# Attention scores computed in four 32-column tiles of TensorE, values product in halves, one output bank for two head groups

## The reference

```python
x = L0_attn_x                                   # 8 x 512 x 128 floats
# attention: 16 heads of dimension 8
h = layernorm(x)
q, k, v = h@Wq.T+bq, h@Wk.T+bk, h@Wv.T+bv       # each 8, 512, 16 heads, 8
a = softmax(einsum('bqhd,bkhd->bhqk', q, k) / sqrt(8))
a = a * head_mask[None, :, None, None]
x = x + einsum('bhqk,bkhd->bqhd', a, v).reshape(8, 512, 128) @ Wo.T + bo
# feed-forward: one shared expert and 8 routed ones (128 -> 512 -> 128), 2 of 8 per token
y = layernorm(x)
probs = softmax(y @ Wr); topk_p, topk_i = top_k(probs, 2); topk_p /= sum(topk_p)
x = x + gelu(y@Wfc_s+b)@Wproj_s+b + sum over the 2 experts of topk_p * (gelu(y@Wfc[e]+b)@Wproj[e]+b)
```

## Time and profile before

| what | value |
|---|---|
| median of three runs | 700.45 us (699.07 to 701.12) |
| profiled execution, its own time | 700.0 us |
| its span, first to last instruction | 698.2 us |
| one batch of attention, in the steady state | 50.3 us |
| attention, first exponential of batch 0 to the end of batch 7 | 76.7 to 472.6 us of the span |
| PE, DVE, ACT, POOL busy over the span | 634, 540, 438, 257 us |

### The profile page before, as it was taken

How to read it: one execution, slowest core, us unless ns; L and a number is a source line. 1 busy time by engine, 2 the same in 40 slices (tenths; PEclk the granted TensorE clock), 3 DMA queues, 4 the chain that set the end, 5 groups by cost and what they waited for, 6 DMA issues and landing times.

```text
span 698.2 us, 13370 instructions
## 1 busy us (share of the span) xinstructions
PE 633.9 (91%) x3934; PEld 324.6 (46%) x3976; DVE 540.3 (77%) x1180; ACT 437.9 (63%) x953; POOL 256.6 (37%) x386
## 2 busy tenths in 40 slices
PE   1766799999999999999999999997979999999996
PEld 1441222323323323323332332323779999998965
DVE  6998778888998998988989989822656666666558
ACT  0881467777687787787787787793425555555541
POOL 6766200020430420421521512506464555454541
PEclk9996799999999999999999999999999999999998
DMA  5399594411311212212221121000112222212174
GB/s 151 93 335 349 126 237 107 115 46 36 92 44 43 83 43 68 69 45 63 63 64 48 58 69 48 21 1 31 47 50 66 66 65 63 68 59 62 47 246 127
DMA packets 67611, 61.28 MB, mean 88 GB/s; under 512 B 16250, under 2 KB 58106, under 8 KB 67562
## 3 DMA queue, kind: packets, MB, share of 16 engines
q1 hardware_dynamic: 63242, 51.79, 26.7%
q0 software_dynamic: 4320, 8.89, 3.8%
HBM read 35.76 MB, written 24.62 MB: 86 GB/s over the span
## 4 chain that ended last, share of the span: by engine, by line
PE 63%; DVE 14%; issue 7%; SPq 5%; POOL 4%; ACT 4%; DMA 3%; DVEq 0%; ACTq 0%; POOLq 0%; another core or an unknown queue 0%
PE ps L1183 13%; PE ps L1172 13%; PE ps L1154 12%; PE ps L1357 10%; PE ps L1369 8%; DVE mx L827 6%; POOL slots L514 2%; DVE x_sb L1097 2%; SPq L295 2%; DMA q_op<-mxT 2%; PE ps L1309 1%; DVE o_t L835 1%; PE ps L1209 1%; PE ps L1317 1%; SPq L305 1%
## 5 line engine op out<-in xcount | busy, mean ns | idle before, releaser
L676 ACT ACTIVATE probs<-ps 128x512 f32<-128x512 f32 x512 | 278.8, 595 | 102.5 <-PE ps L1172 87.8
L827 DVE TENSOR_REDUCE mx<-ps 128x2 f32<-128x1024 f32 x256 | 304.0, 1212 | 42.8 <-PE ps L1154 37.5
L1154 PE MATMUL ps<-k_op,q_op 96*128 96x512 bf16 x512 | 181.5, 394 | 19.2 <-DVE mx L827 7.0
L1172 PE MATMUL ps<-q_op,k_op 128*128 128x512 bf16 x470 | 179.0, 387 | 2.2 <-DMA q_op<-mxT 1.5
L1172 PEld LDWEIGHTS ps<-q_op,k_op 128*128 128x128 bf16 x512 | 49.6, 98 | 187.5 <-ACT probs L676 127.7
L1183 PE MATMUL ps<-probs,v_op 128*32 128x512 f32 x1024 | 136.0, 604 | 0.5 <-issue 0.2
L723 ACT ACTIVATE probs<-ps,b_cur 128x128 f32<-128x128 f32 x284 | 81.4, 368 | 75.7 <-PE ps L1357 65.3
L577 POOL DMA_INDIRECT results<-rest,row_id x71 | 73.9, 1041 | 75.1 <-DVE rest L1041 57.1
L514 POOL DMA_INDIRECT slots<-route_sb,slot_u x64 | 67.0, 1046 | 75.1 <-ACT probs L676 50.8
L1357 PE MATMUL ps<-xn,qk 128*128 128x128 f32 x568 | 79.2, 284 | 3.7 <-DVE xn L1034 1.7
L1154 PEld LDWEIGHTS ps<-k_op,q_op 96*128 96x128 bf16 x512 | 49.5, 99 | 61.7 <-DVE mx L827 27.6
(11 more groups left out here) (135 smaller groups left out, 591.8 us busy)
## 6 DMA issues: line engine op xcount, KB each, us to landing
q_op<-q_scr SPq DMA_DIRECT2D x96, 96.0 KB
k_op<-k_scr SPq DMA_DIRECT2D x96, 96.0 KB
w_sb<-in_W SPq DMA_DIRECT2D x18, 256.0 KB, 4.0
probs<-slots SPq DMA_DIRECT2D x71, 64.5 KB, 1.9
k_scr<-probs SPq DMA_DIRECT2D x16, 256.0 KB, 3.7
q_scr<-probs SPq DMA_DIRECT2D x8, 384.0 KB, 3.1
k_scr<-probs SPq DMA_DIRECT2D x8, 384.0 KB, 3.6
k_scr<-probs SPq DMA_DIRECT2D x16, 128.0 KB, 3.1
```

The source lines that it names most:

```text
L676: nc.scalar.activation(probs[:, i, j, :], ps[:, BK_S + j % key_banks(b, hg), :], ACT.Exp, scale=float(D) ** -0.5).then_inc(s_exp, 1)
L827: nc.vector.reduce_max(mx[:, slot % 2, 2 * p:2 * p + 2], ps[:, bank:bank + 2, :], AX.X).then_inc(s_max, 1)
L1154: last = nc.tensor.matmul(ps[:, BK_A + a % 4, :], q_op[hg][0:SH, j, P * i:P * (i + 1)], k_op[hg][0:SH, j, :], start=True, stop=True)
L1172: nc.tensor.matmul(ps[:, BK_S + j % key_banks(b, hg), :], k_op[hg][:, j, P * i:P * (i + 1)], q_op[hg][:, j, :], start=True, stop=True).the ...
```

## The change

- Every bf16 score matmul (`row_scores`, `key_scores`) becomes four, each with 32 stationary columns, that write four blocks of 32 partitions (`QUARTERS`). The moving operand (512 columns) is the same for all four. `project_out` is cut in the same way, and `max_rows` becomes a matmul with 32 stationary columns.
- `pv` is cut in two halves of 256 queries, eight calls per head group at the steps `PV_SLOTS`, so one half in every second step; `ROW_TILES` now gives two row tiles to steps 0 and 2 of each four.
- Two head groups share bank 6: the ones and values of odd groups lie 16 columns further in `v_op`, and DVE empties the bank once for both. The head mask is multiplied into `wo_sb` once, ahead, by POOL.
- DVE gives up `residual` for batches 0 to 6 and the update of the running count: ACT copies the projection from PSUM to `rest` (L684, step 5 of group 1), POOL adds it (L519 of the changed file) and updates the count (L525).
- `Y_STEPS`, `YT_STEP`, the router's step and the place of `ln2_stats` move.

```diff
-        PV_LAG, MX_STEP, YT_STEP = 11, 7, 13
-        Y_STEPS = (-1, 3, 7, 11)
+        MX_STEP, YT_STEP = 7, 14
+        Y_STEPS = (3, 6, 9, 12)
+        AP_STEP = -11
+        ROUTER_STEP, ROUTER_PAIRS = 3, (2, 3, 4, 5)
-        ROW_TILES = ((0,), (1, 2), (3,), ())
+        ROW_TILES = ((0, 1), (), (2, 3), ())
+        PV_SLOTS = ((11, 12, 13, 15, 17, 19, 21, 23), (9, 11, 13, 15, 17, 19, 21, 23))
+        QUARTERS = [slice(32 * c, 32 * c + 32) for c in range(P // 32)]
...
+            def residual(b):
+                if b == 0:
+                    pool.wait_ge(s_xbo, B)
+                pool.wait_ge(s_apc, b + 1)
+                sl = x_sb[:, b * NT:(b + 1) * NT, :]
+                nc.gpsimd.tensor_tensor(sl, sl, projected[:, :].rearrange("p (n c) -> p n c", c=C), ALU.add).then_inc(s_x2, 1)
...
+            def copy_projection(b):
+                act.wait_ge(s_ap, b + 1)
+                wait(act, s_x2, b)
+                nc.scalar.activation(projected[:, :], ps[:, BK_M, :], ACT.Copy).then_inc(s_apc, 1)
...
-                    nc.vector.scalar_tensor_tensor(out=o_all[:, :, hg, :], in0=o_t[:, :, 1:1 + D],
-                                                   scalar=mask_sb[:, hg:hg + 1],
-                                                   in1=o_rec[:, :].unsqueeze(2).to_broadcast([P, S // 32, D]),
-                                                   op0=ALU.mult, op1=ALU.mult).then_inc(s_onrm, 1)
+                    nc.vector.tensor_tensor(o_all[:, :, 2 * pair:2 * pair + 2, :], both[:, :, :, 1:1 + D],
+                                            o_rec[:, :, :].unsqueeze(3).to_broadcast([P, S // 32, 2, D]),
+                                            ALU.mult).then_inc(s_onrm, 1)
...
-                        if 3 <= p < 7 and hg > 0:
-                            out_norm(b, hg - 1, p - 3)
+                        if 3 <= p < 7 and hg == 2:
+                            out_norm(b, 0, p - 3)
...
-                last = nc.tensor.matmul(ps[:, BK_A + a % 4, :], q_op[hg][0:SH, j, P * i:P * (i + 1)], k_op[hg][0:SH, j, :],
-                                        start=True, stop=True)
+                for c in QUARTERS:
+                    last = nc.tensor.matmul(ps[c, BK_A + a % 4, :], q_op[hg][0:SH, j, P * i + c.start:P * i + c.stop],
+                                            k_op[hg][0:SH, j, :], start=True, stop=True)
...
+                cols = slice(S // 2 * half, S // 2 * (half + 1))
...
                 for j in range(J):
-                    last = nc.tensor.matmul(ps[32 * j:32 * j + 32, BK_O, :], v_op[:, hg, i, j, :], probs[:, i, j, :],
-                                            start=(i == 0), stop=(i == NT - 1))
-                last.then_inc(s_pv, 1)
+                    last = nc.tensor.matmul(ps[32 * j:32 * j + 32, BK_O, cols], v_op[:, hg, i, j, :], probs[:, i, j, cols],
+                                            start=(hg % 2 == 0 and i == 0 and half == 0),
+                                            stop=(hg % 2 == 1 and i == NT - 1 and half == 1))
+                if half == 1:
+                    last.then_inc(s_pv, 1)
```

More of the change, by code:

```diff
@@ L1293, in _ @@
             sequences(attend)
[L1294 to L1295 removed]
+            for k in range(2 * NT):
+                if PV_SLOTS[(HG - 1) % 2][k] >= J * NT:
+                    pv(B - 1, HG - 1, k // 2, k % 2)
             for i in range(NT):
```

134 lines of the change are left out of this document (75 added, 59 removed).

## The result

The changed kernel takes 697.18 us (median of 16 runs, 694.69 to 701.20) against 700.15 (16 runs, 699.07 to 701.12): a ratio of 0.9965, 95% interval 0.9952 to 0.9978. So it is faster by 0.35%, where 3.8% was forecast. The profiled execution took 696.87 us with a span of 695.0.

What follows compares the result with a forecast made beforehand. PE was taken as the bound, busy 49.2 of 50.3 us a batch. Batches 1 to 6 gave 21.6 us, batch 0 2.7, batch 7 1.8 and 0.3: 26.4 together, from 700.0 to a 674 us median, range 662 to 703.

Steps and rivals of the forecast that it cites:

- Edit 1: Attention scores in quarters on PE: 0.22 us a set, cycle 2.95 to 2.61 us, 5.4 us less a batch, 0.7 paid back.
- Rival B: PE not fed fast enough for some 830 records a batch, deciding at 61 ns each: slower, 709 or 733 us; chance 0.15.
- C: Rival: sets of quarters at 0.26 us eat all that PE saves, no change at 700 us; chance 0.05.
- D: Rival: quarters do not run side by side, 0.66 us more a set, 1300 us; chance 0.03.
- Edits 2 and 3: Attention: halves and row tiles shrink ACT's waits at no PE cost; DVE falls from 45.1 to 42.0 us a batch.
- The 1.1 us that I charged to group 0 for VectorE: Group 0 of each batch: DVE needs 11.6 us against PE's 10.4 plus 0.1, making a batch 46.7 us.
- Edit 4: Work moved to ACT and POOL is hidden; scales come 3.3 us into group 2, ACT wants them at about 3.2.
- rival A: Gain partly given back: sets cost 0.24 us or scales come 2 us late for ACT; 685 to 688 us; chance 0.16.
- the sum: Whole kernel: six batches at 3.6 us, batch 0 and both halves of batch 7 added, 26.4 us less in all.
- the half batch: First half of batch 7 in attention: 1.8 us less.
- batch 0: First batch of attention: 2.7 us less, between half and all of 3.6, as its first groups may wait for something else.
- the second half of batch 7: End of attention, without row scores and bounded by ACT: 0.3 us less.

Runs made afterwards that it cites:

- e3: Changed kernel with normalising activations at steps 6, 8, 10, 12 instead of 3, 6, 9, 12: 664.41 us, ratio 0.9624, where the kernel before took 689.55.
- e4: Changed kernel with the last batch's output projection as four whole-array matmuls instead of sixteen of 32 columns: 670.94 us, ratio 0.9731, on an early chip.
- e14: Changed kernel with VectorE's statistics one pair of maxima earlier, normalising steps unaltered: 686.30 us, ratio 0.9844, on a late chip.
- a0: Changed kernel unaltered, measured once more on a late chip: 696.41 us, ratio 0.9951 to the kernel before.
- e7: Changed kernel with normalising at steps 6, 8, 10, 12 and the last projection as four whole-array matmuls: 687.72 us, ratio 0.9805, on a late chip.
- a0c: Changed kernel unaltered, measured again on another late chip: 694.36 us, ratio 0.9928 to the kernel before.
- e15: Changed kernel with statistics one pair of maxima earlier and the last projection as four whole-array matmuls: 685.07 us, ratio 0.9793, on a late chip.
- c1: Kernel before with its 64 scatters moved out of attention to behind it (another output): 765.83 us, ratio 1.1106, on an early chip.

## Why the prediction was wrong, step by step

- **Edit 1** held: sets at 0.22 us, a cycle of 2.60 (2.61 said), the passages at 0.09 to 0.14 us. Rival B was wrong: 201 records in 10.7 us are 53 ns each, under the 61 at which it decides. Nor does the supply set even that pace: the 32 records of the projection (e3's L1250) take 1.08 us in all, under 34 ns each. C and D fell with it.
- **Edits 2 and 3** held in sum: with no late signal and no late scales (e3) a batch takes 46.54 us, 46.7 said, and ACT's waits for key scores fall from 10.3 to 4.2 us a batch; VectorE is busy 42.8 us in the four windows (42.0), ACT 40.3 (38.6). The 1.1 us that I charged to group 0 for VectorE did not fall there (10.7 us, 11.6 said); VectorE is idle there for just 0.2 us, and for 1.0 in group 1, so it probably carries the surplus over. The sum came out right partly by luck, because group 2, which I had left to PE, takes 11.93 with PE busy for 11.55.
- **Edit 4**, "hidden by a hair; each us by which it is late costs one in each batch": late by 0.9 us, and it cost 0.9 to 1.1 in each of seven batches, 6.8 us (groups 2 of e4 against e3). The scales came when I said, 3.2 us into group 2 (3.3 said). The term that was mis-sized is when ACT asks for them: its four exponentials follow each other at 0.6 us, so it is ready 2.4 us into the group, not 3.2 (e14's first normalisation starts there, with the scales ready). The mechanism and its price stood in the text; it is part of rival A.
- **The step that failed** is the sum, which multiplied the 3.6 us of one undisturbed batch by six, and the half batch likewise, and took the part behind attention as unchanged, as if a signal always came as fast as in the earlier trace rows. The scatters appear in it only as POOL's busy time, 14.2 us a batch and harmless; what they do to TensorE's signals was put at nothing. On the chips of the first measurement they hold them up, by up to 1.3 us in the short cycle, which costs 2.2 to 2.5 us a batch of the 3.6.

The account against the forecast's 26.4 us (span before and after: 3.1 gained, 23.3 missing), in differences between the traces. Missing: in batches 2 to 6, groups 0 and 1 take 122.7 us where 5 x 22.2 are undisturbed, 11.7; the same in batch 7, 2.3; the part behind the last exponential is 4.3 longer; late scales 6.8; a start 1.2 us later (it varies by 2 us between runs); the rest of the second half of batch 7, 0.7. Against these, batch 0 is better by 1.7 than I took it, and the undisturbed batches by 2.0 in all. Late signals are thus 14.0 us inside attention, and with those behind it some 16 to 18 of the 23 us. The tail's share is the least certain part: POOL begins its scales there 3.6 us later than before, but whole-array matmuls took back only 2.1 us (a0 to e7) and 2.3 (a0c to e15), and on the two other late chips the changed kernel's tail is 228.7 and 228.6 us.

On an early chip the change should take e3's 664.4 + 6.8 = 671 us, near e4's time, or 0.973 of the kernel before: 18 or 19 us of the 26.4. That is an estimate, and the unaltered kernel was not measured there.

Open: what a late chip has that an early one hasn't, and by which way a scatter holds up TensorE's signals (its issue on GpSimd and its transfers were only moved together). The quarters were never tried without the halves, nor VectorE's lighter load alone. On late chips some semaphore records are missing, so the counts of late signals are lower bounds. All executions carried the profiler; whether one without it shows the same wasn't tried.

## What to carry to other kernels

A stage shortened until its engines hand over without slack pays in full for every late signal that slack used to hide; look in the trace for what runs beside it (here GpSimd's scatters) and compare a batch that has it with one that hasn't, before multiplying one cycle's gain by the number of cycles. Keep TensorE in one column-tiled form through a whole stage or not at all: each passage cost 0.09 to 0.14 us here, and every half-converted stream was slower than the kernel before. A hand-over that is computed to be met by a tenth of a us should be moved by one step at once: here that cost nothing and gave back 7 us.

## What the hardware showed that I had not expected

Late chips lose time behind attention as well, in either kernel, and there with whole-array matmuls alone. The 71 scatters of results by line: the kernel before on the late chip of the first measurement, and on an early one (c1, which is the same kernel behind attention but for the scatters moved there); the changed kernel, and e3.

```profile
L577 POOL DMA_INDIRECT results<-rest,row_id x71 | 73.9, 1041 | 75.1 <-DVE rest L1041 57.1
```

```profile
L572 POOL DMA_INDIRECT results<-rest,row_id x71 | 71.7, 1010 | 67.0 <-DVE rest L1035 49.1
```

```profile
L602 POOL DMA_INDIRECT results<-rest,row_id x71 | 73.4, 1033 | 76.3 <-DVE rest L1071 58.4
```

```profile
L602 POOL DMA_INDIRECT results<-rest,row_id x71 | 71.5, 1008 | 67.6 <-DVE rest L1071 49.8
```

The scatters themselves differ by 25 to 31 ns each, but POOL waits 8.1 and 8.7 us more between them. The timelines show by what. The first layer of an expert, whole-array fp32 matmuls with a scatter beside them, and the activation that reads them, in the kernel before on the late chip:

```profile
530.05 0.98 POOL L577 DMA_INDIRECT results<-rest,row_id  x1 [0.31 <-issue]
530.26 1.06 PE L1357 MATMUL ps<-xn,qk 128*128 128x128 f32 x8
...
531.76 1.14 ACT L723 ACTIVATE probs<-ps,b_cur 128x128 f32<-128x128 f32 x4 [1.55 <-PE ps L1357]
```

The same in e3, on an early chip:

```profile
508.91 0.96 POOL L602 DMA_INDIRECT results<-rest,row_id  x1 [0.30 <-issue]
509.40 1.06 PE L1399 MATMUL ps<-xn,qk 128*128 128x128 f32 x8
510.05 1.14 ACT L756 ACTIVATE probs<-ps,b_cur 128x128 f32<-128x128 f32 x4 [0.67 <-PE ps L1399]
```

The reader starts 1.50 us behind the first matmul in the one and 0.65 in the other. By the semaphore records 119 of some 290 signals of such matmuls come 0.15 us or more late in the kernel before on the late chip (half of these by 0.37 us or more, at most 1.6), 124 in the changed kernel, and 2 in c1 and in e3. So late signals are no peculiarity of the 32-column form or of the changed kernel: beside scatters a late chip has them in either kernel, and the attention of the kernel before, with nothing late on record, is the exception.

From the last exponential to the end late chips need 226 to 232 us and early ones 218 to 220. POOL's longer waits and scatters come to 10.3 us in the kernel before, which is about the 10.6 us by which its time itself differs between the first measurement and the first early chip; a ratio to a kernel measured on another chip would have been off by 1.5%, four times what the change was worth here.
